# An eight-layer transformer kernel on one core: its table of step orders searched anew, with a layout that charges for a change in the rows or columns used between two products

## What is computed

```
x = x + L0_xattn(ctx, ctx, ln(x), ...)            # one head
x = x + L0_ffn(ln(x), ...)                        # SwitchHead: 8 heads x 8 experts, top 2, gated
x = x + L1_xattn(ln(x), ctx, ctx, masks, ...)     # 16 heads of 8
x = x + L1_ffn(ln(x), ...)                        # ternary weights, 512 hidden, gelu
x = x + L2_xattn(ln(x), ctx, mask, ...)           # 2 heads of 64, per-head layer norm
x = x + L2_ffn(ln(x), ...)                        # 8 experts, top 2, gelu
x = x + L3_xattn(ln(x), ctx, ctx, bias, ...)      # 16 heads of 64
x = x + L3_ffn(ln(x), ...)                        # 8 experts in groups, top 2, plus a shared part
```

## Time and profile before

| what | value |
|---|---|
| time before, median of 3 runs | 684.0 us (683.98 to 688.49) |
| time of the profiled execution | 684.11 us |
| its span, first to last instruction | 682.8 us |
| mean granted TensorE clock | 0.989 |
| PE busy | 654.7 us (96%), 5566 records |
| DVE, ACT, POOL busy | 523.3, 372.4, 203.6 us |
| transfers | 113.86 MB |

### The profile page before, as it was taken

The page is one execution under the profiler, slowest core; times in us unless marked ns, Lnnn a source line. Parts: engine busy times, 40 slices in busy tenths (PEclk is TensorE's granted clock), DMA queues, the critical chain, the costliest instruction groups (busy, mean ns, idle before and its releaser), DMA issues.

```text
span 682.8 us, 14844 instructions
## 1 busy us (share of the span) xinstructions
PE 654.7 (96%) x5566; PEld 589.5 (86%) x5566; DVE 523.3 (77%) x1433; ACT 372.4 (55%) x1261; POOL 203.6 (30%) x244
## 2 busy tenths in 40 slices
PE   6889999999999999999999999999999998899898
PEld 5779999788989999998799998987899997669776
DVE  1987587995788889895788999887588866657756
ACT  2251421356664866236655686377647653966683
POOL 0010002832331422304424242135232532533140
PEclk9999999999999999999999999999999999899999
DMA  8979969987312916885346027577026500000000
GB/s 319 395 237 306 401 233 314 330 291 244 129 62 69 329 33 219 271 298 204 102 150 228 2 66 221 188 234 234 33 55 232 201 16 5 1 1 1 1 1 13
DMA packets 37655, 113.86 MB, mean 167 GB/s; under 512 B 9040, under 2 KB 11728, under 8 KB 37200
## 3 DMA queue, kind: packets, MB, share of 16 engines
q1 hardware_dynamic: 37584, 112.92, 47.9%
HBM read 111.86 MB, written 1.05 MB: 165 GB/s over the span
## 4 chain that ended last, share of the span: by engine, by line
PE 78%; DVE 12%; ACT 6%; DMA 2%; issue 1%; POOL 1%; DVEq 0%
PE bank L462 35%; PE e_bank L462 31%; PE p_bank L462 5%; PE bank L713 3%; ACT wide_b L1136 3%; DVE gated L1442 2%; DVE wide_b L1445 1%; DMA gated<-gates_of 1%; POOL wide_b L1346 1%; DVE max_neg L1728 1%; PE bank L702 1%; DVE f_route L1442 1%; ACT f_b L1045 1%; PE p_bank L562 1%; ACT wide_a L995 1%
## 5 line engine op out<-in xcount | busy, mean ns | idle before, releaser
L462 PE MATMUL e_bank<-weights,gated 128*128 128x128 f32 x2048 | 246.9, 277 | 0.3 <-ACT f_v L995 0.2
L462 PEld LDWEIGHTS e_bank<-weights,gated 128*128 128x128 f32 x2048 | 236.6, 192 | 8.2 <-issue 4.0
L1346 POOL TENSOR_TENSOR wide_b<-wide_b,row_inv 128x480 f32<-128x480 f32 x64 | 76.0, 1196 | 132.5 <-DVE row_inv L1733 132.4
L1136 ACT ACTIVATE wide_b<-wide_b,max_neg 128x120 f32<-128x120 f32 x272 | 103.5, 386 | 19.0 <-DVE max_neg L1728 16.3
L995 ACT ACTIVATE wide_a<-bank 120x512 f32<-120x512 f32 (+4 forms) x110 | 59.0, 545 | 50.9 <-PE bank L713 23.3
L1442 DVE TENSOR_TENSOR gated<-gated,f_xnT 128x1024 f32<-128x1024 f32 x64 | 81.9, 1302 | 6.3 <-DMA gated<-gates_of 5.8
L1442 DVE TENSOR_TENSOR gated<-gated,f_v 128x1024 f32<-128x1024 f32 x64 | 78.8, 1250 | 8.5 <-ACT f_v L995 4.2
L1338 POOL TENSOR_TENSOR rstd<-var_eps,w_const 128x1 f32<-128x1 f32 (+1 forms) x48 | 34.4, 717 | 144.6 <-DVE var_eps L1438 144.5
L1136 ACT ACTIVATION_READ_ACCUMULATOR wide_b<-wide_b,max_neg 128x1 f32 x272 | 52.3, 192 | 0.0
L713 PE MATMUL bank<-w_const,wide_b 128*120 128x128 f32 x256 | 40.4, 284 | 3.8 <-POOL wide_b L1346 3.7
L1728 DVE TENSOR_REDUCE max_neg<-wide_b 128x4 f32<-128x480 f32 x64 | 41.8, 653 | 2.2
(11 more groups left out here) (265 smaller groups left out, 1229.7 us busy)
## 6 DMA issues: line engine op xcount, KB each, us to landing
gated<-gates_of SPq DMA_DIRECT2D x128, 512.0 KB, 5.8
weights<-in_experts SPq DMA_DIRECT2D x64, 512.0 KB, 6.4
w_L2f<-in_L2f SPq DMA_DIRECT2D x1, 2124.0 KB, 14.6
w_L3x<-in_L3x SPq DMA_DIRECT2D x1, 2108.0 KB, 18.6
wide_b<-in_raw0f SPq DMA_DIRECT2D x1, 1024.0 KB, 7.9
w_L3f<-in_L3f SPq DMA_DIRECT2D x1, 1000.0 KB, 21.1
w_L1f<-in_L1f SPq DMA_DIRECT2D x1, 516.0 KB, 10.9
x_next<-in_x SPq DMA_DIRECT2D x4, 128.0 KB, 6.4
```

The source lines that it names most:

```text
L462: return nc.tensor.matmul(o, lhsT, rhs, start=first, stop=last)
L1136: last = nc.scalar.activation(p, p, ACT.Exp, bias=max_neg[lane][:, h:h + 1], accum_out=row_sum[lane][:, h:h + 1])
L1346: nc.gpsimd.tensor_tensor(p3, p3, row_inv[lane][:, 4 * i:4 * i + 4].unsqueeze(2).broadcast_to([128, 4, K]), ALU.mult).then_inc(probs_norme ...
```

## The change

The five strings of `ORDER` are replaced by others that a new search found; its layout charges for a change in the rows or columns of the array used from one product to the next. Steps, instructions, waits, tiles and transfers are the same. A few lines of the diff stand for it, since the letters tell little:

```
 ORDER = {
-    "PE": "pppp0pp00pp0pppp0pp00pp0pppp0pffpffpfpfffpfffpf0pffffpfpfpfpfpffffpfffffpffffpfffpp0p101p0pfffpf1f0f"
...
+    "PE": "pppp0pp000pppppp0pp00pp0pppp0ffffpfpfpfpfp0fffpfpffffpfpfpfpfpffffffpffpfffffpfffpp010p101p0fpfff1pf"
...
```

More of the change, by code:

```diff
@@ L44 @@
 ORDER = {
[L45 to L57, removed]
@@ L65 @@
[L65 to L68 removed]
+    "PE": "pppp0pp000pppppp0pp00pp0pppp0ffffpfpfpfpfp0fffpfpffffpfpfpfpfpffffffpffpfffffpfffpp010p101p0fpfff1pf"
+          "fffp0fpf0pf00f10000f00f0ffp00f00f1p0fp0fp00101p110f00f00p10101101001f10p10f1001f01f11f0fp1f0f1p11f10"
+          "11001001110p0101f111pf10ff100f1p11p0101p01f1f0f0f1fffpf1pff11pff1010fp1ff1f01f00pf10f1010f1p1fp1110f"
+          "101f1100p110p10f100p10f10pf11001p0fff0f100010p110f110010010p0100101ff101110f01p00f1f001p1010010101f1"
+          "1f0pf010f010f01ff10p1f1p01f01010f00f00f100f0f100f00110f01100101f11f01001101f01f101f00f11f100f1011101"
+          "10001011f1f0f101f01110f10f01101f010011f1f11010f1f1f0f101ff1011f0011ff1f1100f1101f1001010100110110101"
+          "00ff10011f0ff0fff11100f0111010000000100101f0101001010101001010ff01011101ff110100110f0f11",
@@ new lines @@
+    "Activation": "ppppp0p0p00ppppp00pppppppppfppp00pfp0fpfpfpfpfpfppp0p0p0ppp010p1p01pf00pf0p0p01010f10000010f0f0p0f0p"
+          "fpf01010p1101p00p1100111p010110101p001p01010101010010pp10p00111101p001111p1110p10101f10pp1f001p11f0p"
+          "101pf0f0101f10f111fp110110p10101110p110p10010p101pp10001p01101010p000p01p010100100110010p1011101010p"
+          "010111001f00p11010pf101000100100100f0110p0100101f1001110f1011f01f110f1010110111010100100000101100110"
+          "1110110111001010111101101011111100110100011100101010010110101010011001100110000010010100010001100010"
+          "110101111110010011101",
@@ new lines @@
+    "DVE": "pppppp0p0pppppp0p0pppppppppppppffpffpppffpffppfffppfffpfppfpppfffffppfppffpfpfpppfpppff0ffpfppfffp0p"
+          "10fffp1fpf0f0ff10ffp000fp01pff1100f1f00fp1000f010f0f00fpp1p010ff00000pf00pp111010pfppp1f10f0f01p01pp"
+          "10101f01pfp0f1p11pf1p1011p10pp0f011010011p1100p1f00fff1fpff0111fff011f0pf10ffff111f0pff100100p111111"
+          "1p01pffff10pp0fp1f1p00f01p1fp10f10101fp0010p1pp0f1101p1pp010p1ppf00001p0001f1p1001f00000110fp11f11p1"
+          "fpp10ffp0f000010f0f10110ff01f1f01f101100f0100ff01011ff1f100111f00f000100100101101ff01f010100ff001011"
+          "001f11111f01010100f0011ff01111111f01ffff0010f001110110110101f10ff10111111010100000101110101001001011"
+          "010011001111000010100010001100000001101111101000000001111111110101",
@@ L69 @@
+    "Pool": "pppp011001f010fpf001001000p1010100110010110010001101111111f10pf0f001010111p1000111101010001010101100"
+          "0011f1f1010000100101010011f0110110011001000101110111101f110111010f0f0011100101010100010000111011",
+    "SP": "pppfffffffffpfffffffffffffffffffffpfffffffffpfffffffpffffffffffffffff0fffpfffffffffp1pfffffffff0ffff"
+          "ffffffffffff1ff0ffffffpfffff1ffffffffffffpfffff10ff0fffff1fffff0f011ff",
 }
```

11 lines of the change are left out of this document (removed).

## The result

The new order is slower: 690.5 us median (687.14 to 693.48, four executions) against 684.25 us for the kernel before on the same chip, a ratio of 1.0085 with a 95% interval of 1.0064 to 1.0105 (the quotient of the two medians is 1.0092). The forecast was 680.6 us with a range of 677.0 to 685.5. The profiled execution took 687.14 us, its span is 685.8 us.

A forecast was written before the change was run, and what follows sets the result against it. PE was taken as the bound from 45 to 572 us, busy 522.3 of 527.0 us. From 684.1 us, 2.5 for changes of shape and 1.0 for the end were subtracted, giving 680.6, range 677.0 to 685.5.

The forecast's parts named there:

- Changes of shape removed: PE up to the last front unit: thirteen fewer tile-shape changes at 0.19 us, 2.5 us gained, bounds 2.0 to 2.6.
- rival (a): Middle: shape changes go but time returns as waits on other engines; only the end gains, 683.1 us; chance 0.17.
- Everything else that is moved: All other reordering on all engines: taken as 0, bounds -2.3 to +4.7 us from the middle's idle time.
- The clock: Last stretch: TensorE low spells dealt out differently, 1.7 to 3.4 us either way per spell, inside a term taken as 0.
- The end of the program: Last two lanes: routing fills DVE's idle time, lane 1's mixing starts earlier; 1.0 us gained, bounds 0 to 1.9.
- Rival (c): Last softmax: PE meets POOL, lane 1 late by 3.5 us plus 3.4 of low clock; 687.5 us; chance 0.12.
- Rival (b): New search also removes half the middle's waits and one low clock spell in the last stretch; 676.6 us; chance 0.14.

The follow-up runs named there:

- e18: e4's kernel with six PE steps moved between 130 and 565 us, taking out ten changes of tile shape; 684.1 us, ratio 0.9990.
- e9: Kernel before, with one of eight expert products in each of 64 units using 64 rows, adding 128 changes of shape; 706.7 us, ratio 1.0327.
- e13: As e9 on the kernel before, but four products in a row per unit use 64 rows, same 128 added changes; 707.1 us, ratio 1.0337.
- e5: Kernel after with the 120 to 150 us block and SP's load order up to there put back to old; 685.0 us, ratio 1.0005.
- e15: Kernel after with two short DVE steps near 125 us moved earlier and SP's early load order; 686.7 us, ratio 1.0034.
- e14: Kernel after with only two short DVE steps near 125 us moved earlier; 688.4 us, ratio 1.0058.
- e11: Kernel before with one SP step, the second pair's x and context loads, moved behind five other transfers; 689.0 us, ratio 1.0076.
- e1: Kernel after with only the 120 to 150 us block in the old order, loads still late; 690.9 us, ratio 1.0097.
- e12: Kernel after with only SP's string in the old order up to 150 us, so the load is early; 688.0 us, ratio 1.0046.
- e7: Old order to about 150 us on all engines, new order behind it; 685.8 us, ratio 1.0022 against the kernel before.
- e16: Kernel after with ten unread identity turns on PE ahead of each lane's L1_xattn scores, first pair only; 688.0 us, ratio 1.0065.
- e3: New order to the end of the front at 576 us, old order behind it; 691.6 us, ratio 1.0114 against the kernel before.
- e4: Old order to the end of the front at 576 us, new order behind it; 682.2 us, ratio 0.9969 against the kernel before.
- e19: Same kernel as e4, repeated as the control of e18; 682.6 us, ratio 0.9971.
- e17: Kernel before with one DVE exchange: lane 1's last five routing instructions ahead of lane 0's mixing; 683.7 us, ratio 0.9992.
- e10: Kernel of e5 with one DVE step near 236 us, lane 0's fourth row_inv, moved ahead of three others; median 685.2 us.
- e2: Kernel before with only the 120 to 150 us block in the new order; 691.9 us, ratio 1.0106.
- e8: Old order to about 290 us on all engines, new order behind it; 688.2 us, ratio 1.0058 against the kernel before.

## Why the prediction was wrong

**Changes of shape removed, -2.5 us.** The price was right: 0.19 taken, 0.175 to 0.182 measured when changes are added. The term was wrong as it stood alone, because it took a price for a gain. From the 640th to the 1024th expert product the new order has seven changes fewer, worth 7 x 0.18 = 1.3 us, and takes 0.7 us more; PE's waits above 0.25 us there grew from 1.6 to 3.7 us, so the saved changes are there and the new waits are larger. e18 shows the same with ten changes chosen by hand. This is rival (a), held at 0.17, and its argument against itself was the flaw: "these 4.7 us are all the waiting there is, so 522.3 us are PE's own". That PE is full in the old order says only that this order covers every answer with work of PE. It doesn't say that PE alone sets the pace: take work out, and the answers that it covered come too late. A change added lengthens PE's own line and nothing covers it, so e9 and e13 see the full price.

**Everything else that is moved, 0 (bounds -2.3 to +4.7).** This is the step that failed by its size. The middle lost 4.8 us in the profiled execution where 2.5 were to be gained, 7.3 us off. The rows account for it: PE's idle time between the 256th and the last expert product rose from 4.3 to 9.6 us, and the low spell cost 1.7. The bound was "as much again", 4.7 us, and had no term for the clock in the middle. The largest part is the block of 120 to 150 us: e5 takes back 5.5 us together with the load. In it are two short DVE steps behind two products that POOL stretches; with the early load their repair gives 3.8 back (e15), alone it isn't told apart from nothing (e14). The late load costs 5.2 us in the old kernel (e11) and 5.9 with the old block (e1 against e5). In the new order no engine waits for it, because DVE's step that reads it stands later; it shows only once the block is repaired. So neither repair alone gives more than half: e1 nothing, e12 2.6 by the medians, both together 5.5. My comparison, "13 before and 17 after have under 0.85 us of work between", counted PE's own work between a product and its answer. It could see neither what stood ahead of the answer on DVE's queue nor SP's queue, of which the prediction says nothing.

**The clock.** I had let it fall only in the last stretch. In the middle some of these waits bring a low spell of 3.4 us or more, which costs half of its length where PE is full: behind the two waits of 1.2 us in after 3.4 us, behind the 2.92 us in e11 6.8, behind the 1.9 us near 240 us only in e1 and e7, and behind 1.65 and 0.84 us in e15 none. e16 shows in the block that this is a cost apart from the idle time, 1.7 us. It may be a part of why the medians are worse than the profile: after's profiled execution, 687.14 us, was its fastest of four. It isn't all: another of the four had the same mean clock of 0.990 and took 689.63 us. e3 has the same order up to 576 us; in its execution the low spell of the block is 6.8 us long and the 256th to the 640th product take 199.4 us, not 197.4. What the other three executions of after did was not seen.

**The end of the program, -1.0 us (bounds 0 to -1.9).** The mechanism held and the size was 1.8 us (e4, and e19 again), near the upper bound. The rows of the end of after:

```profile
677.24 0.17 DVE L1442 TENSOR_TENSOR route<-route 128x8 f32<-128x8 f32 x1
...
678.72 0.76 DVE L1442 TENSOR_TENSOR wide_b<-bank,gate 128x256 f32<-128x256 f32 x2 [0.46 <-PE bank L462]
680.77 0.76 DVE L1442 TENSOR_TENSOR wide_b<-bank,gate 128x256 f32<-128x256 f32 x2 [0.23 <-PE bank L462]
```

Against the earlier trace rows: the routing ends ahead of lane 0's mixing at 678.72, and lane 1's mixing follows 2.05 us later instead of 2.78. That is 0.73 us, near the 0.85 of the term, and e17 alone gives 0.65 by the medians, within the noise. The other 1.1 us come from further up in the tail, where no run looked by itself.

**Rival (a), 683.1 us.** Its mechanism is what e7, e10 and e18 show. Its number assumed that the waits give back just what the changes gain; they give back more.

**Rival (c), slower by PE meeting POOL in the last softmax.** The wait came as described:

```profile
646.62 1.16 PE L462 MATMUL bank<-wide_b,wide_a 64*128 64x120 f32 x16
647.70 1.16 PE L462 MATMUL bank<-xnT,w_L3x 128*128 128x128 f32 x8
651.68 0.91 PE L713 MATMUL bank<-w_const,wide_b 128*120 128x128 f32 x4 [2.82 <-POOL wide_b L1346]
```

2.82 us where the earlier trace rows had 1.74. Yet the tail is 1.8 us shorter and the clock in that stretch is 0.90 as before: ACT is busy 16.24 of 17 us there and sets the pace, so the wait has cover. What made the change slower was a place that no rival had named, though it is of the kind of (a).

**Rival (b)** found no support: PE's idle time in the middle doubled instead of halving.

**The chances.** 0.03 for slower by over 1% rested on the worst of (c). The change came out 0.64 to 1.05% slower: within 1% on the median, and 5 us above the top of the range.

What stays open: e5 still stands 2.7 us above e4 with the block and the loads repaired. 0.7 of it is the stretch from the 640th product, and about 2.3 the one before it, of which e10 removed the largest wait without a gain in the median, and of which 0.92 us is the wait at the seam. Why one kernel's executions spread as they do is not settled: e5 683.4 to 686.9, e16 686.5 to 692.9, e4 681.7 to 682.9, but the kernel before too had one of 689.4 among 23; their mean clocks explain only part.

## What to carry to other kernels

On a nearly full engine, the price of an overhead, even if measured well, is what one more of it costs; one less gives it only where nothing else comes late by the move that saves it. Before counting a gain, ask for each removed piece which answer of another engine it had covered, and look at the queue of that engine, the DMA issuer's included, not at distances on the full engine. In a new order look first where the stages change over: there the loads, the short steps that release two lanes and the low clock meet. And when one block is put back alone to find a cause, look for waits that neither whole order has: the splice can make them (e2, e8), and two delays can hide each other (e1).

## What the runs showed that was not expected

Two idle gaps of 1.2 us within 4 us of PE were followed by 3.4 us of the lower clock in an engine that is 95% busy, and with 20 identity products of 0.11 us in those gaps the profiled execution had no such spell and was 1.7 us shorter over the block. A gap of 1.9 us had a low spell behind it in two of nine executions. Two DVE products of 128x128, with two inputs each, together took 2.21 us beside POOL's `wide_a` instead of 0.62 us. A product with 64 rows costs PE the same as one with 128 (e13 against e9: 192 of them, 0.9 us more, not less), so what the 64-row products cost beyond full ones is in the changes of shape.
